# Three sums of input blocks moved from VectorE to GpSimd, once, at the start of a two-stage fp32 kernel

## The reference, cut to what matters

```
x = x + conv(x masked to its length, 64 kernels of 1024 taps) + D * x, masked again
gate = x @ W_gate.T + 0.5 * (x @ A_gate[r].T) @ B_gate[r].T       # F = 2752
up   = x @ W_up.T   + 0.5 * (x @ A_up[r].T)   @ B_up[r].T
act  = silu(gate) * up
x = x + act @ W_down.T + 0.5 * (act @ A_down[r].T) @ B_down[r].T
```

## Time and profile before

| | |
|---|---|
| time of the runs | 1717.09, 1717.53, 1723.28 us, median 1717.53 us |
| time of the profiled execution | 1715.87 us |
| its span in the profile | 1714.2 us |
| PE busy | 1628.6 us, 95% of the span |
| DVE, ACT, POOL busy | 920.5, 566.1, 114.4 us |
| convolution | to about 200 us |
| prologue of the first sweep and tile 0 | 202.7 to about 260 us |

### The profile page before, as it was taken

The page is one execution under the profiler, slowest core; times in us unless marked ns, Lnnn a source line. Parts: engine busy times, 40 slices in busy tenths (PEclk is TensorE's granted clock), DMA queues, the critical chain, the costliest instruction groups (busy, mean ns, idle before and its releaser), DMA issues.

```text
span 1714.2 us, 21064 instructions
## 1 busy us (share of the span) xinstructions
PE 1628.6 (95%) x8224; PEld 1394.1 (81%) x8224; DVE 920.5 (54%) x1182; ACT 566.1 (33%) x678; POOL 114.4 (7%) x185
## 2 busy tenths in 40 slices
PE   2989989999999997899999999998999999999999
PEld 2988878888888886778888888886888888888887
DVE  6544686665566664876665666666325325325322
ACT  2211353333333332543333333334224224224211
POOL 5100022442120000000000000000000000000000
PEclk9999989999999998999999999999999999999999
DMA  8989654664453335233333333328448547547542
GB/s 309 366 327 334 222 188 145 194 201 157 148 166 98 99 99 187 90 93 99 98 99 98 99 99 99 99 74 273 133 134 248 148 140 241 163 133 227 174 139 60
DMA packets 156869, 278.40 MB, mean 162 GB/s; under 512 B 55554, under 2 KB 72770, under 8 KB 156226
## 3 DMA queue, kind: packets, MB, share of 16 engines
q1 hardware_dynamic: 104034, 234.19, 42.5%
q0 software_dynamic: 12672, 25.82, 4.8%
q10 hardware_dynamic: 40064, 17.04, 3.5%
HBM read 237.26 MB, written 65.31 MB: 177 GB/s over the span
## 4 chain that ended last, share of the span: by engine, by line
PE 87%; DMA 5%; DVE 4%; issue 2%; ACT 1%; SPq 0%; DVEq 0%; ACTq 0%
PE ps L806 81%; PE ps L791 6%; DMA tt<-k_pad 2%; DMA k_pad<-ksb 1%; DMA raw<-a_gu_sel 1%; DVE xlo L1523 1%; ACT whi L1001 1%; DMA xraw<-x_keep 1%; DVE wlo L1523 1%; DVE xraw L1523 1%; DMA draw<-act_keep 0%; DVE xres L1717 0%; ACT lohi L1001 0%; ACT cc L1001 0%; DMA leni<-len 0%
## 5 line engine op out<-in xcount | busy, mean ns | idle before, releaser
L806 PE MATMUL ps<-xhi,whi 128*128 128x512 f32 (+1 forms) x1080 | 421.2, 390 | 29.7 <-ACT cc L1001 10.5
L806 PE MATMUL ps<-xlo,whi 128*128 128x512 f32 (+1 forms) x1080 | 419.9, 389 | 0.0
L806 PE MATMUL ps<-xhi,wlo 128*128 128x512 f32 (+1 forms) x1080 | 418.7, 388 | 0.0
L1001 ACT ACTIVATE whi<-raw 128x1024 fp32r<-128x1024 f32 (+3 forms) x202 | 198.1, 981 | 580.8 <-PE ps L806 546.7
L1523 DVE TENSOR_TENSOR wlo<-raw,whi 128x1024 fp32r<-128x1024 f32 (+1 forms) x190 | 219.4, 1155 | 307.0 <-ACT whi L1001 306.7
L806 PE MATMUL ps<-dhi,whi 128*128 128x512 f32 (+2 forms) x760 | 288.0, 379 | 3.7 <-DVE xres L1717 3.7
L806 PE MATMUL ps<-dlo,whi 128*128 128x512 f32 (+2 forms) x760 | 286.6, 377 | 0.0
L806 PE MATMUL ps<-dhi,wlo 128*128 128x512 f32 (+2 forms) x760 | 286.4, 377 | 0.0
L806 PEld LDWEIGHTS ps<-xhi,whi 128*128 128x128 f32 x1080 | 206.7, 191 | 69.6 <-DVE gq L1645 10.1
L806 PEld LDWEIGHTS ps<-xhi,wlo 128*128 128x128 f32 x1080 | 206.1, 191 | 41.5
L806 PEld LDWEIGHTS ps<-xlo,whi 128*128 128x128 f32 x1080 | 206.6, 191 | 37.4
(11 more groups left out here) (174 smaller groups left out, 1663.8 us busy)
## 6 DMA issues: line engine op xcount, KB each, us to landing
raw<-wgu SPq DMA_DIRECT2D x84, 512.0 KB, 6.7
tt<-k_pad SPq DMA_DIRECT2D x64, 512.0 KB, 8.6
raw<-wd SPq DMA_DIRECT2D x64, 512.0 KB, 3.8
loraw<-bgu_sel SPq DMA_DIRECT2D x84, 256.0 KB, 4.5
act_keep<-up SPq DMA_DIRECT2D x42, 512.0 KB, 3.1
draw<-act_keep SPq DMA_DIRECT2D x84, 256.0 KB, 6.9
raw<-wd SPq DMA_DIRECT2D x32, 320.0 KB, 3.0
xr<-xr SPq DMA_DIRECT2D x4, 2048.0 KB, 10.5
```

The source lines that it names most:

```text
L806: return nc.tensor.matmul(out, w, x, start=start, stop=stop, skip_group_check=True)
L1001: return nc.scalar.activation(out, in_, ACT.Copy)
```

## The change

In the first sweep, T3, T2 and T4 are no longer formed by DVE but by GpSimd. GpSimd does it after its second group of gathers and ahead of `gather_rest(0)`. It waits for the end of the last evacuation of the convolution and for the second part of T1 (which DVE still makes), and from T3 to T2 to T4 it waits for its own preceding result. The three instructions count on the same semaphore. The second sweep is as before.

```diff
--- before.py
+++ after.py
@@ -756,6 +756,13 @@
             gather_gu(0, FIRST)
             pool.wait_ge(s_gat, GU_SEL)
             gather_gu(1, FIRST)
+            pool.wait_ge(s_cev, H)
+            pool.wait_ge(s_xform, xform(0, "T1", "post"))
+            for q, a, b, op in (("T3", "B22", "B12", ALU.subtract), ("T2", "T3", "B11", ALU.add), ("T4", "B21", "T2", ALU.subtract)):
+                if q != "T3":
+                    pool.wait_ge(s_xform, xform(0, a if a in TS else b))
+                nc.gpsimd.tensor_tensor(part_of(x_in(0, q), "all"), x_source(0, a, "all"), x_source(0, b, "all"),
+                                        op).then_inc(s_xform, 1)
             pool.wait_ge(s_p, prod(0, "P1"))
             pool.wait_ge(s_gat, 2 * GU_SEL)
             gather_rest(0)
@@ -1737,9 +1744,6 @@
             x_form(0, "T1", "post")
             w_lo("agB0", 0)
             w_lo("agB1", 0)
-            x_form(0, "T3")
-            x_form(0, "T2")
-            x_form(0, "T4")
             x_lo(0, "T1", "post")
             t_mask(0, "A")
             t_lo(0, "A")
```

## The result

The changed kernel took 1721.61 us (median of 20 runs, 1720.40 to 1727.07), the kernel before, over 20 runs, 1718.51 us (1716.88 to 1723.28): 3.1 us slower, ratio 1.0018, 95% interval 1.0011 to 1.0025, that is 1.9 to 4.3 us. The profiled execution has a span of 1721.5 us. Its convolution happened to end 3.14 us later than in the trace of before (last evacuation at 203.32, not at 200.18), which the change doesn't touch.

The account below looks back on a forecast made before the run. PE, busy 95%, was taken as the bound, its long run's start set by ACT's train from T4 hi. With turns T4 hi moves from 234.9 to 239.1, +4.2; 1717.5 + 4.2 = 1721.7 us, range 1716 to 1729.

Parts of the forecast that it names:

- The duration of a sum: Each 128 x 2048 sum on GpSimd, undisturbed: 4.4 us, the middle of 3.5 and 5.2 us.
- the slow case: GpSimd sums in the first sweep take 9.8 us each, D = +17.2, 1734.7 us; chance 0.10.
- T4: Last GpSimd sum, which gates the load of `bl`: done at 225.9 us, with GpSimd and DVE excluding each other.
- The turns: GpSimd sums and DVE's tile reads alternate whole instructions, the waiting one first: D = +4.2; chance 0.50.
- "side by side" rival: GpSimd sums and DVE run undisturbed: T4 done at 223.15, D = +1.0, 1718.5 us; chance 0.30.
- The train: ACT's fixed sequence from T4 hi: adapter tile's hi 6.08 us later, `cc` 10.38 us later, both shifting by D.
- no longer the last: Load of `bl` ahead of T4 hi: landed at 228.8, so it no longer decides; tlo B starts at 230.65.
- The wait ahead of P1: PE waits 2.5 us for u0 lo, eating the 4.10 us stretch and not adding to D.
- A wait ahead of P5: PE waits for u1 lo, eating the 4.10 us stretch and not adding to D; no separate size given.
- The gain refused: Prologue, 7.03 us taken off DVE: T3 hi waits for PE, so the gain is at most 1.0 to 1.1 us.
- The clock: PE's slow stretch after the wait for `cc`: 2.5 us lost before as after, 0 to 2 us more allowed.
- The time changes behind `cc`: Sign of being wrong: PE's time after `cc` was to stay the same for 200 us.

Follow-up runs that it names:

- memset experiments: Changed kernel with its three GpSimd sums replaced by memsets, three each or one each: +1.35 us and -1.28 us against the kernel before.
- writes-only kernel: Changed kernel with each GpSimd sum replaced by three memsets of about the sum's length, reading no tile: ratio 1.0007 to the kernel before.
- last kernel above: Kernel before with T4's split behind the adapter tile, `cc` straight after it and the stores' wait moved from ACT to DVE: ratio 0.9972.
- sums for nothing: Changed kernel with each GpSimd sum replaced by one memset, so T4 is ready early: ratio 0.9990 to the kernel before.
- T4 alone: Changed kernel with T3 and T2 back on DVE and only T4 on GpSimd: ratio 1.0001 to the kernel before.
- one sum more: Changed kernel with T3 formed twice on GpSimd: ratio 1.0048 to the kernel before.
- T4 split later: Kernel before with T4's split moved behind the adapter tile of n = 0 on ACT and DVE, sums on DVE: ratio 0.9986.

## Why the prediction was right, and where a term was off

The forecast was 1721.7 us, the time is 1721.6. That the two meet within 0.1 us is luck, a match of two small errors (last two points), so the steps count for more.

- **The duration of a sum** was taken as 4.4 us from the middle of two bounds; it is 4.46 to 4.49. The memset of 2048 columns, 1.7 us by the slope, took 1.81 in the memset experiments. (The 9.8 us of the slow case should be 9.6, three times 3.2; nothing hangs on it.)
- **T4.** Predicted at 225.9 on the clock of the trace of before; measured 229.02 - 3.14 = 225.88. The turns came in the order given: `wlo`, T2, `xlo`, T4, with the mask free. By the rule of the Trainium skill (SBUF — State Buffer, Who interferes with whom), named in the prediction, the later one is blocked for a whole instruction: the traces agree, at 5.13 us for a `wlo` of 1.23 us. The "side by side" rival falls with it, as the writes-only kernel shows what it would have looked like.
- **The train.** tlo B was foreseen at 230.65, measured 233.56 - 3.14 = 230.42, with the load of `bl` "no longer the last", as said, by 0.4 us. T4 hi was foreseen at +4.2, measured +4.02; the adapter tile's hi +4.01; `cc` +3.94. The wait ahead of P1 was foreseen at 2.5 us, measured 2.4. A wait ahead of P5 was foreseen too, and there was none in PE's list. PE ran at granted clock 0.51 behind the wait ahead of P1 and came to P5 at 240.92, 1.7 us later still, when u1 lo was done (240.35). So PE's wait for the adapter tile did not shrink as foreseen. The prediction had `cc` wait for the stores of `rest_parts`, where the earlier trace rows names PE; it was right in that: in the changed kernel the second store landed at 252.17 and `cc` started at 252.32, and in the last kernel above, where that wait was moved, `cc` came straight behind the adapter tile.
- **The gain refused.** "Not below -1.1": with the sums for nothing, -0.86 at T4 hi and -1.28 in time.
- **The clock, the term that was off in the trace.** I took the slow stretch of P6 as the same before and after (2.5 us lost), with 0 to 2 us more in the range. It became shorter. In P6's window PE ran at 0.50 from 246.40 to 251.70 before, 13 matmuls, and from 253.49 to 256.70 after, 8 matmuls. They start 0.43 us apart there, not 0.23, so 5 fewer are 1.0 us, and the shift fell from +3.94 at `cc` to +2.96 at the first read of P4. "The time changes behind `cc`" was one of the prediction's own signs of being wrong, and it came, with 1.0 us. At 0.2 us each, the count of matmuls 0.43 us apart accounts for most of the step between these two columns of the table in the other kernels as well, except the last, where DVE's first sum of the banks holds P4: 4 slow matmuls fewer than before give -0.94 (writes only), 2 fewer -0.44 (T4 alone), 3 fewer -0.67 (one sum more), 6 fewer -1.21 (T4 split later), 2 more +0.35 (sums for nothing). What sets the count stays open: it was not varied by itself, and with one trace for each kernel it may go with the execution and not with the kernel.
- **The baseline.** The sum was made on 1717.5; over 20 runs the kernel before is at 1718.5. That is the other error: +4.2 on 1717.5 and +3.1 on 1718.5 give the same. By itself the +4.2 lies within the interval of the difference, 1.9 to 4.3, near its upper end.

## What to carry to other kernels

Before giving work from DVE to GpSimd, look at what DVE does at the time. Where it reads two tiles, each GpSimd instruction that reads a tile holds it up until it has ended: here 3.1 to 4.4 us a sum, to save 2.3. Before moving work off a busy engine, ask which single wait ends last there: here 7 us less on DVE were worth 1 us, while moving one split and one wait in the order, with no work taken away, gave 4.8. And a result that frees space (T4 frees `xt`) has followers that no data dependence shows; look for who waits to write there.

## What the runs showed of the hardware that was not expected

- A blocked DVE instruction counts as busy in the profile: DVE's busy time rose from 920.5 to 924.9 us, although 6.9 us of work had left it. In the changed kernel no list of waits names GpSimd for it, and the chain of waits runs through DVE (`xlo` for 5.10 us). Only the duration of the instruction beside its usual one gives the block away.
- The turns went one instruction each, in the order in which the records start. The next sum starts in the profile while DVE's blocked instruction is still under way (218.50, against 219.43 for the following `xlo`), so it stands ahead of DVE's next one, though that was ready. In the kernel with one sum more this held over four sums.
- A GpSimd memset doesn't disturb DVE (1.22 us for `wlo` beside it), a GpSimd copy of 1.75 us does (2.33 us).
